# Three edits to a perceiver kernel: the first tile's border, the last self group, the first gate chunk

## The chip, the cores and the metric

The kernel runs on one core of a Trainium2 chip. The metric is the device time of one execution in microseconds (us); the time before the change is 1605.65 us, the median of 3 runs (1605.06 to 1606.41).

## The reference

One perceiver block in f32 over x of 64 batches x 32 queries x 512. Every part adds to x:

```python
x = x + xattn(layernorm(x), ctx_768)   # 16 heads of 64, 257 keys of 384 per batch, q @ k.T / 8, softmax, @ v, @ Wo + bo
x = x + attn(layernorm(x))             # 32 keys per batch, relative position bias, softmax, @ v, @ Wo
x = x + ffn(layernorm(x))              # gate, up: 512 -> 1408, silu(gate) * up, down: 1408 -> 512
```

In the ffn the input, the hidden and all three weights are rounded to 8 bits: the scale of an activation is its largest absolute value over the whole tensor, that of a weight row its own. So no gate product can start before the last token of the second residual is normed and its maximum taken.

## The kernel before

The 2048 tokens are 16 tiles of 128 (4 batches each) and 4 groups of 4 tiles. The stages follow each other: the query projections of all groups (the result, `qk_by_tile`, goes to DRAM and comes back a tile at a time as `raw`); cross attention tile by tile (tile 0 "first", tile 1 "second", tiles 2 to 14 a loop, tile 15 "last", then a tail); self attention group by group; the ffn. f32 products are done as three products of high and low parts, so each operand is split: ScalarE (ACT) copies the high part, VectorE (DVE) subtracts to get the low part. Each engine's instructions stand in a written order, and semaphores join the engines: `filled` and `drained` count the uses of each of the 8 PSUM banks (s0, s1, t0, t1, o0, o1, q0, q1).

A cross tile works on four batches b = 0 to 3. For each, TensorE (PE) does four score products (L651, one bank each), transposes the probabilities of the batch before (L662), multiplies them with that batch's context (L674, three pieces, called PV here), and transposes the context of the batch ahead (`ctxT`, L620, chunks 0, 1, 2 in banks t0, t1, t0). DVE takes row maxima (L1151), splits the transposed probabilities (L935, pT) and contexts (L935, cT), scales half of the probabilities (L1159, norm) and adds the last key's part to PV's result (L1136, attended). GpSimd (POOL) subtracts each batch's last key from its context (`pool_less_last`, L1258) and splits the context into high and low (`pool_split`, L1273 and L1276). SyncE (SP) issues every DMA, in order, from one queue.

At the border of two tiles (b = 3) the next tile's `raw` is split into `qk`: four pieces rg = 0 to 3, high by ACT (L797), low by DVE (L1070, `dve_qk_low`). The score products of the next tile wait for these pieces (`s_qlo`) and, for rg = 0, for the three cT chunks. In tile 0 the order at the border is its own, since no output projection (`pe_wo`, L702) of a tile before stands there: `qk_next and not begun` in `dve_cross_tile`.

In the self part a group's last step goes over its tiles i = 0 to 3: `pe_self_attended` (L1505, 64 small products into four banks), products for later v (`pe_self_v`, L1491), `pe_self_out` (L1520, 24 products of 512 columns). The result of attended must be split by ACT and DVE into `aT2` before the out product reads it; there is one `aT2`. DVE then adds the residual (`x_res2`, one tile, loaded by SP) in `dve_self_out` (L1725), and norms. In the last group the norms go straight to `xn3_all`, while the 12 tiles of the earlier groups come back from DRAM in one load (L1929).

In the ffn `pe_gate_up` does 11 chunks of gate and up products for 512 tokens (L1963), three rounds in a loop and a last one. The tokens come in two halves of 256, each transposed by PE (L1951) into q0 and q1; for the first round DVE copies half 0 to `xqT` (L2093) and ACT half 1 (L2029). Before its first product a round waits for both:

```python
            for b in ("q0", "q1"):
                pe.wait_ge(drained[b], U3.before(b, n, section, 1))
```

## Time and profile before

| | |
|---|---|
| median of 3 runs | 1605.65 us (1605.06 to 1606.41) |
| profiled execution, its own time | 1601.76 us |
| its span, first to last instruction | 1600.0 us |
| PE busy | 1548.1 us, 97% |
| DVE busy | 1072.9 us, 67% |
| ACT busy | 732.2 us, 46% |
| POOL busy | 372.2 us, 23% |
| mean granted TensorE clock | 0.988 |

PE is busy almost everywhere, so time is lost only where it stands still or runs at a lower granted clock. The page's row of 40 slices shows these places: the first slice, the slices from 160 to 240 us (end of the projections and tile 0 of cross attention), and 1440 to 1480 us (end of self attention and start of the ffn), where the granted clock is 0.79 of full speed in the mean.

### The profile page before, as it was taken

The page shows a single profiled execution, that of the slowest core. Times are in us where ns is not written, and L with a number is a line of the kernel's source. Part 1 is how long each engine was busy: PE and PEld are TensorE (multiplying, and loading weights), DVE is VectorE, ACT ScalarE, POOL GpSimd, SP SyncE. Part 2 cuts the span into 40 slices and gives each one's busy share as a digit, 9 for nine tenths or more (in the row PEclk, how much of TensorE's full clock was granted, in tenths as well). Part 3 has the DMA queues.
Part 4 walks back from the last instruction along what each step waited for, and adds up shares of the span by engine and source line. Part 5 has one row for each costly group of instructions (what it writes and reads, how often), then busy time and mean ns, then how long its engine had stood idle before and what let it go on. Part 6 is the DMA issues. An engine that isn't in the chain of part 4 may idle for free.

```text
span 1600.0 us, 36060 instructions
## 1 busy us (share of the span) xinstructions
PE 1548.1 (97%) x13778; PEld 1286.6 (80%) x13778; DVE 1072.9 (67%) x2314; ACT 732.2 (46%) x1589; POOL 372.2 (23%) x225
## 2 busy tenths in 40 slices
PE   7999879999999999999999999999999999996989
PEld 6888668888989899888989899878878788784444
DVE  7766677776667766776667766556565565555788
ACT  5544645555545554555545554433222222223755
POOL 1000343343444344343444344400000000000000
PEclk9999989999999999999999999999999999997999
DMA  6898862431333223331334223240311312242022
GB/s 245 319 366 327 330 243 109 137 135 59 138 132 140 74 106 136 136 134 59 138 134 138 76 104 122 97 181 22 120 54 40 114 41 66 100 157 97 1 105 106
DMA packets 80047, 213.63 MB, mean 134 GB/s; under 512 B 5776, under 2 KB 31824, under 8 KB 77136
## 3 DMA queue, kind: packets, MB, share of 16 engines
q1 hardware_dynamic: 79952, 212.27, 36.9%
q8 instruction: 71, 1.16, 0.3%
q14 instruction: 24, 0.20, 0.0%
HBM read 141.86 MB, written 70.39 MB: 133 GB/s over the span
## 4 chain that ended last, share of the span: by engine, by line
PE 74%; issue 11%; DVE 9%; ACT 4%; DMA 1%; POOL 0%; DVEq 0%; SPq 0%; ACTq 0%; POOLq 0%
PE psum_o L674 13%; PE psum_s L651 7%; PE psum_q L651 6%; PE psum_o L1451 6%; PE psum_q L1491 6%; PE psum_q L1451 6%; PE psum_t L1520 6%; PE psum_o L539 5%; PE psum_o L689 5%; DVE qk L1070 3%; PE psum_t L662 3%; PE psum_t L620 2%; PE psum_s L1478 1%; PE psum_t L571 1%; PE psum_q L571 1%
## 5 line engine op out<-in xcount | busy, mean ns | idle before, releaser
L674 PE MATMUL psum_o<-pT,c_nat 128*128 128x512 f32 x1152 | 307.3, 403 | 1.0 <-DVE pT L935 0.7
L674 PEld LDWEIGHTS psum_o<-pT,c_nat 128*128 128x128 f32 x1152 | 202.7, 188 | 36.1 <-DVE pT L935 1.0
L1273 POOL TENSOR_TENSOR c_nat<-c_raw,constants 128x768 fp32r<-128x768 f32 x64 | 94.9, 1483 | 574.4 <-PE psum_o L674 460.3
L1136 DVE TENSOR_SCALAR oT<-psum_o,c_last 128x512 f32<-128x512 f32 x192 | 143.9, 749 | 66.7 <-PE psum_o L674 66.6
L651 PE MATMUL psum_s<-cT,qk 128*128 128x256 f32 (+1 forms) x1152 | 168.8, 289 | 11.2 <-DVE cT L935 9.3
L651 PEld LDWEIGHTS psum_s<-cT,qk 128*128 128x128 f32 x1152 | 152.1, 191 | 20.3 <-DVE cT L935 14.1
L864 ACT ACTIVATE probs<-psum_s,nmax 128x257 f32<-128x257 f32 x128 | 61.1, 477 | 205.2 <-DVE nmax L1151 205.2
L651 PE MATMUL psum_q<-cT,qk 128*128 128x256 f32 (+1 forms) x1152 | 152.2, 283 | 0.7 <-DVE qk L1070 0.7
L651 PEld LDWEIGHTS psum_q<-cT,qk 128*128 128x128 f32 x1152 | 143.0, 190 | 3.5 <-issue 2.6
L935 DVE TENSOR_TENSOR pT<-psum_t,pT 128x512 fp32r<-128x512 f32 x128 | 87.8, 687 | 70.9 <-ACT pT L755 70.9
L1258 POOL TENSOR_TENSOR c_raw<-c_raw,last_row 128x768 f32<-128x768 f32 x64 | 120.2, 1879 | 22.2 <-DMA last_row<-in_ctx_dram 22.2
L755 ACT ACTIVATE cT<-psum_t 128x256 fp32r<-128x256 f32 x192 | 67.1, 387 | 115.3 <-PE psum_t L620 115.2
L1276 POOL TENSOR_TENSOR c_nat<-c_raw,c_nat 128x768 fp32r<-128x768 f32 x64 | 118.1, 1846 | 5.0
L1070 DVE TENSOR_TENSOR qk<-raw,qk 128x1536 fp32r<-128x1536 f32 x62 | 108.1, 1765 | 0.0
L2215 POOL PARTITION_ALL_REDUCE tiny<-tiny x1 | 0.4, 381 | 445.3 <-DVE tiny L2131 445.3
L797 ACT ACTIVATE qk<-raw 128x1536 fp32r<-128x1536 f32 x64 | 94.6, 1515 | 0.0
L689 PE MATMUL psum_o<-oT,wv 128*64 128x128 f32 x1536 | 87.4, 274 | 0.2 <-issue 0.2
L539 PE MATMUL psum_o<-xnT,wq 128*128 128x512 f32 x372 | 87.2, 393 | 0.0
L1520 PE MATMUL psum_t<-w2o_high,aT 128*128 128x512 f32 x256 | 83.0, 396 | 4.0 <-DVE aT L935 4.0
L689 PEld LDWEIGHTS psum_o<-oT,wv 128*64 128x64 f32 x1536 | 83.5, 137 | 2.4 <-issue 0.4
L1491 PE MATMUL psum_q<-w2v_high,xnT 128*128 128x512 f32 x256 | 84.6, 397 | 0.0
L539 PEld LDWEIGHTS psum_o<-xnT,wq 128*128 128x128 f32 x372 | 69.1, 188 | 17.1 <-issue 1.4
(273 smaller groups left out, 3120.3 us busy)
## 6 DMA issues: line engine op xcount, KB each, us to landing
qk_by_tile<-staged SPq DMA_DIRECT2D x32, 1536.0 KB, 10.2
raw<-qk_by_tile SPq DMA_DIRECT2D x16, 3072.0 KB, 12.3
c_raw<-in_ctx_dram SPq DMA_DIRECT2D x64, 384.0 KB, 3.2
last_row<-in_ctx_dram SPq DMA_DIRECT2D x64, 192.0 KB, 3.9
out_dram<-x_out SPq DMA_DIRECT2D x32, 256.0 KB, 2.0
x_res<-in_x_dram SPq DMA_DIRECT2D x16, 256.0 KB, 2.7
x_in<-out_dram SPq DMA_DIRECT2D x4, 1024.0 KB, 8.3
x_res<-out_dram SPq DMA_DIRECT2D x16, 256.0 KB, 2.9
```

The costliest lines, as they stand in the source:

```text
L539: m = pe.matmul(ps[:], wq[:, part, k, j * P:(j + 1) * P], xnT[:, moving, k, :, :], start=(k, part, moving) == (0, 0, 0), stop=(k, part) == ...
L651: m = pe.matmul(ps[:, 0:keys], qk[:, part, rg, c, b, :], cT[b % 2][:, moving, c, 0:keys], start=(c, part, moving) == (0, 0, 0), stop=(c, p ...
L674: i = pe.matmul(ps[:], c_nat[(b - 1) % 2][:, part, k, m * P:(m + 1) * P], pT[:, moving, k, :], start=(k, part, moving) == (0, 0, 0), stop= ...
L689: i = pe.matmul(ps[64 * par:64 * par + 64, h4 * P:(h4 + 1) * P], wv[:, c, head * DH:(head + 1) * DH], oT[:, c, slot, :, :], start=c == 0, ...
L1070: nc.vector.tensor_tensor(part[1], raw[:, :, rg, :].rearrange("p h (a q) -> p h a q", q=SQ), part[0].bitcast(F32), ALU.subtract).then_inc( ...
L1136: nc.vector.tensor_scalar(oT[:, m, :, (b - 1) % 4, :], ps[:].rearrange("p (s q) -> p s q", q=SQ), c_last[:, (b - 1) % 2, m:m + 1], None, A ...
L1258: nc.gpsimd.tensor_tensor(c_raw[i][:], c_raw[i][:], row_, ALU.subtract).then_inc(s_sub, 1)
L1273: G.tensor_tensor(flat(c_nat[i][:, 0, :, :]), flat(c_raw[i][:]), zero.to_broadcast([P, 2 * DC]), ALU.add).then_inc(s_chi, 1)
L1276: G.tensor_tensor(c_nat[i][:, 1, :, :], c_raw[i][:], c_nat[i][:, 0, :, :].bitcast(F32), ALU.subtract).then_inc(s_nat, 1)
L1451: m = pe.matmul(ps[:], (w2_high[w], w2_low[w])[part][:, k, j * P:(j + 1) * P], xnT2[:, moving, k, :, :], start=(k, part, moving) == (0, 0, ...
L1491: m = pe.matmul(ps[:], xnT2[:, part, k, i, :], w[moving][:, k, 512 * n:512 * (n + 1)], start=(k, part, moving) == (0, 0, 0), stop=(k, part ...
L1520: m = pe.matmul(ps[:], aT2[:, part, k, :], w[moving][:, k, :], start=(k, part, moving) == (0, 0, 0), stop=(k, part) == (KI - 1, 1))
```

## The change

Four things move; no product is added or taken away, except that some are cut in two.

1. Border of tile 0. DVE's order is new: piece 0 of `qk` first, then attended 0, chunks 0 and 1 of the context, piece 1, the norms, chunk 2, attended 1, pieces 2 and 3. ACT copies context chunk 2 ahead of pieces 2 and 3. In tile 1 POOL waits until all four `qk` pieces are split, and does `pool_less_last` of batch 1 ahead of `pool_split` of batch 0.
2. SP issues Wo, Wv, bo and x_res behind the context of batch 4 (tile 1's first).
3. Last self group. The last v product moves behind attended(2), out(2) is cut in two halves of 12 products, and attended(3) stands between them; tile 3 has a buffer of its own (`aT2_last`), and the residuals of tiles 2 and 3 come in one load (`x_res_last`). DVE does the probabilities of tile 3 earlier, and the norms of tiles 0 and 1 before the split of tile 3. Both buffers lie where `xn3_all` will be, so the load of the normed groups is cut: group 0 where all three stood, groups 1 and 2 behind the last tile's store, with a wait of its own on ACT before the gate loop.
4. Gate chunk 0 of each loop round is done in two passes of 256 tokens, and the first needs only half 0.

```diff
@@ act_cross_tile
+                if b == 3 and not begun:
+                    ctxT(b, 2)
...
-                if after:
+                if after and (b < 3 or begun):
                     ctxT(b, 2)
@@ dve_cross_tile
-                if qk_next and begun:
+                if qk_next:
                     dve_qk_low(dve, t + 1, 0, section)
                 dve_attended(dve, t, b, 0, section)
                 inverse(b, 3)
-                if qk_next and begun:
+                if qk_next and not begun:
+                    ctxT(b, 0)
+                    ctxT(b, 1)
+                    dve_qk_low(dve, t + 1, 1, section)
+                    norm(b, 2)
+                    norm(b, 3)
+                    ctxT(b, 2)
+                    dve_attended(dve, t, b, 1, section)
+                    dve_qk_low(dve, t + 1, 2, section)
+                    dve_qk_low(dve, t + 1, 3, section)
+                    dve_attended(dve, t, b, 2, section)
+                    continue
@@ pool_cross_tile
+                if section == "second" and b == 0:
+                    pool.wait_ge(s_qlo, 4 * t + 4)
+                    pool_less_last(pool, t, b + 1)
+                    pool_split(pool, t, b, section)
+                    continue
@@ sp_project_all
-            sp.dma_start(wo_raw[:], Wo.rearrange("(k p) n -> p k n", p=P)).then_inc(s_wo, 16)
             full(sp, U1(("CT", 0, 2), 0, "first"))
             sp.wait_ge(s_nat, 2)
             load_ctx(sp, 0, 3)
             load_qk(sp, 0, 1)
+            sp.wait_ge(s_nat, 3)
+            load_ctx(sp, 0, 4)
+            sp.dma_start(wo_raw[:], Wo.rearrange("(k p) n -> p k n", p=P)).then_inc(s_wo, 16)
             sp.dma_start(wv[:], Wv.rearrange("(k p) n -> p k n", p=P)).then_inc(s_wvo, 16)
@@ pe_self_all
+                if last:
+                    pe_self_attended(pe, s, 2)
+                    pe_self_v(pe, s, 3, 1)
+                    pe_self_out(pe, s, 2, range(KI // 2))
+                    pe_self_attended(pe, s, 3)
+                    pe_self_out(pe, s, 2, range(KI // 2, KI))
+                    pe_self_out(pe, s, 3)
@@ dve_self_all, last group
+                    dve_self_probs(dve, s, 3, ch)
+                    dve_self_out(dve, s, 1, ch2)
+                    dve_self_attended(dve, s, 2)
                     dve_out_rsqrt(dve, slice(0, 2), ch2)
                     dve_out_norm(dve, s, slice(0, 2), ch2)
+                    dve_self_attended(dve, s, 3)
+                    dve_self_out(dve, s, 2, ch2)
                     dve_short_rsqrt(dve, 2, ch2)
                     dve_out_norm(dve, s, slice(2, 3), ch2)
+                    dve_self_out(dve, s, 3, ch2)
@@ sp_self_all
                     if not more and i == 0:
+                        sp.dma_start(x_res_last[:], x1_dram[(TILES - 2) * P:, :].rearrange("(t p) d -> p t d", p=P)).then_inc(s_xres_last, 16)
...
+                        sp.dma_start(xn3_all[:, 0:GROUP, :].rearrange("p t d -> p (t d)"), xn3_dram[0]).then_inc(s_x3back, 16)
+                    if not more and i == GROUP - 1:
+                        sp.dma_start(xn3_all[:, GROUP:GROUP * (GROUPS - 1), :].rearrange("p (s t) d -> p s (t d)", t=GROUP),
+                                     xn3_dram[1:].rearrange("s p n -> p s n")).then_inc(s_x3later, 16)
@@ pe_gate_up
+            first = 1 if section == "loop" else 0
+            places = [empty(pe, U3(("GU"[w], i), n, section)) for i in range(first) for w in range(2)]
+            for half, b in enumerate(("q0", "q1")):
                 pe.wait_ge(drained[b], U3.before(b, n, section, 1))
+                for i in range(first):
+                    for w in range(2):
+                        ps, done = places[2 * i + w]
+                        m = products(i, w, ps, slice(256 * half, 256 * half + 256))
+                        if half:
+                            m.then_inc(done, 1)
@@ act_ffn
             act.wait_ge(s_out, 16 + 32 * TILES)
+            act.wait_ge(s_x3later, 16)
             with act.Fori(0, NCH - 1) as n:
```

How DVE's instructions stand at the border of tile 0, before (`qk` is a piece's low part, `cT_90` a context chunk, `probs_65` a norm, `oT` attended, `nmax` the next tile's first row maximum):

```order
269 L1155 RECIPROCAL rden<-den 128x1
270 L1136 TENSOR_SCALAR oT<-psum_o,c_last 128x16x32
271 L1155 RECIPROCAL rden<-den 128x1
272 L935 TENSOR_TENSOR cT_90<-psum_t,cT_90 128x256 x2
273 L1070 TENSOR_TENSOR qk<-raw,qk 128x4x12x32 x2
274 L1159 TENSOR_SCALAR probs_65<-probs_65,rden 128x256 x2
275 L1136 TENSOR_SCALAR oT<-psum_o,c_last 128x16x32
276 L1070 TENSOR_TENSOR qk<-raw,qk 128x4x12x32 x2
277 L935 TENSOR_TENSOR cT_90<-psum_t,cT_90 128x256
278 L1136 TENSOR_SCALAR oT<-psum_o,c_last 128x16x32
279 L1151 TENSOR_REDUCE nmax<-psum_s 128x1
```

And DVE at the same place after the change:

```order
269 L1163 RECIPROCAL rden<-den 128x1
270 L1078 TENSOR_TENSOR qk<-raw,qk 128x4x12x32
271 L1144 TENSOR_SCALAR oT<-psum_o,c_last 128x16x32
272 L1163 RECIPROCAL rden<-den 128x1
273 L943 TENSOR_TENSOR cT_90<-psum_t,cT_90 128x256 x2
274 L1078 TENSOR_TENSOR qk<-raw,qk 128x4x12x32
275 L1167 TENSOR_SCALAR probs_65<-probs_65,rden 128x256 x2
276 L943 TENSOR_TENSOR cT_90<-psum_t,cT_90 128x256
277 L1144 TENSOR_SCALAR oT<-psum_o,c_last 128x16x32
278 L1078 TENSOR_TENSOR qk<-raw,qk 128x4x12x32 x2
279 L1144 TENSOR_SCALAR oT<-psum_o,c_last 128x16x32
280 L1159 TENSOR_REDUCE nmax<-psum_s 128x1
```

The instructions are the same; one piece moved ahead of attended 0, and context chunk 2 from the end to a place before attended 1.

DVE in the last self group before, from the probabilities of tile 3 (`sum`, `pr`, `pT_1`) over out(2) (`x_out`) and the split of attended(3) (`aT_124`) to the norms of tiles 0 and 1 (`xn_all`):

```order
1024 L1701 TENSOR_REDUCE sum_129<-pr_114 128x16
1025 L1702 RECIPROCAL sum_129<-sum_129 128x16
1026 L1703 TENSOR_TENSOR pr_114<-pr_114,sum_129 128x512
1027 L1708 STREAM_TRANSPOSE pT_1_116<-pr_114 128x512
1028 L1725 TENSOR_TENSOR x_out_55<-psum_t,x_res_126 128x512
1029 L1727 BN_STATS out_stats<-x_out_55 128x6
1030 L935 TENSOR_TENSOR aT_124<-psum_s,aT_124 128x8x32 x2
1031 L935 TENSOR_TENSOR aT_124<-psum_o,aT_124 128x8x32 x2
1032 L1756 TENSOR_SCALAR xn_all<-x_out_55,out_ln 128x512 x2
1033 L1762 TENSOR_REDUCE xmax<-xn_all 128x1 x2
```

DVE there after the change; here `x_out` is that of out(1), and `aT_124` the split of attended(2):

```order
1003 L1739 TENSOR_REDUCE sum_129<-pr_114 128x16
1004 L1740 RECIPROCAL sum_129<-sum_129 128x16
1005 L1741 TENSOR_TENSOR pr_114<-pr_114,sum_129 128x512
1006 L1746 STREAM_TRANSPOSE pT_1_116<-pr_114 128x512
1007 L1769 TENSOR_TENSOR x_out_55<-psum_t,x_res_126 128x512
1008 L1771 BN_STATS out_stats<-x_out_55 128x6
1009 L943 TENSOR_TENSOR aT_124<-psum_s,aT_124 128x8x32 x2
1010 L943 TENSOR_TENSOR aT_124<-psum_o,aT_124 128x8x32 x2
1011 L1017 TENSOR_TENSOR out_ln<-out_stats 128x2
```

The probabilities of tile 3 moved ahead of out(1) and of the split of attended(2), which now stands before the reciprocal roots (`out_ln`) of tiles 0 and 1.

## Rows read from the trace of the kernel before

**Rows 1.** Waits of PE: waiting line, releaser, total us, times, longest.
```profile
PE psum_s L651 <- DVE cT L935: 9.3, 1, 9.3
...
PE psum_t L1520 <- DVE aT L935: 4.0, 2, 2.0
```

**Rows 2.** PE's timeline, tiles 0 and 1: start, us, line, idle before.
```profile
240.96 1.01 PE L651 MATMUL psum_s<-cT,qk 128*128 128x256 f32 x3 [9.29 <-DVE cT L935]
...
246.89 1.56 PE L674 MATMUL psum_o<-pT,c_nat 128*128 128x512 f32 x6
...
255.91 5.46 PE L689 MATMUL psum_o<-oT,wv 128*64 128x128 f32 x96
```

**Rows 3.** DVE's timeline at the border of tile 0.
```profile
225.13 0.16 DVE L1155 RECIPROCAL rden<-den 128x1 f32<-128x1 f32 x1 [0.18 <-ACT probs L864]
...
232.19 3.44 DVE L1159 TENSOR_SCALAR probs<-probs,rden 128x256 f32<-128x256 f32 x2
```

**Rows 4.** DVE's timeline at a border in the loop of tiles.
```profile
335.36 1.76 DVE L1070 TENSOR_TENSOR qk<-raw,qk 128x1536 fp32r<-128x1536 f32 x1
...
340.09 0.61 DVE L1159 TENSOR_SCALAR probs<-probs,rden 128x256 f32<-128x256 f32 x2
...
344.60 0.69 DVE L1144 TENSOR_TENSOR x_out<-psum_q,x_res 128x512 f32<-128x512 f32 x1
...
346.35 0.42 DVE L1151 TENSOR_REDUCE nmax<-psum_s 128x1 f32<-128x257 f32 x1
...
348.83 0.68 DVE L935 TENSOR_TENSOR pT<-psum_t,pT 128x512 fp32r<-128x512 f32 x1
```

**Rows 5.** The chain that ended last, in tile 0: start, us, what.
```profile
213.19 12.16 DMA last_row<-in_ctx_dram
```

**Rows 6.** POOL's timeline at the border of tile 0.
```profile
231.04 2.56 POOL L1273 TENSOR_TENSOR c_nat<-c_raw,constants 128x768 fp32r<-128x768 f32 x1 [3.79 <-PE psum_o L674]
...
235.44 1.85 POOL L1258 TENSOR_TENSOR c_raw<-c_raw,last_row 128x768 f32<-128x768 f32 x1
```

**Rows 7.** Windows of 2 us: busy per engine, then granted clock, DMA share, GB/s.
```profile
196.00:198.00 2.00, 0.14 (x2) 0.00 (x0) 1.33 (x4) 0.66 (x3) 2.00 (x2) 1.00 0.98 398
...
200.00:202.00 2.00, 2.00 (x11) 2.00 (x11) 0.95 (x2) 0.42 (x1) 0.00 (x0) 0.50 0.53 98
202.00:204.00 2.00, 2.00 (x15) 2.00 (x15) 1.29 (x5) 1.22 (x4) 0.00 (x0) 0.77 0.98 315
```

**Rows 8.** The chain that ended last, end of the last self group.
```profile
1430.89 5.44 PE psum_t L1520 x24
1436.33 2.72 PE psum_q L1491 x12
1442.50 7.07 PE psum_t L1520 x24
1452.96 5.72 PE psum_t L1520 x24
```

**Rows 9.** DVE's timeline in the last self group.
```profile
1437.82 0.16 DVE L1009 TENSOR_TENSOR out_ln<-out_stats 128x2 f32<-128x2 f32 x1
...
1441.61 0.75 DVE L935 TENSOR_TENSOR aT<-psum_o,aT 128x256 fp32r<-128x256 f32 x2
```

**Rows 10.** Timelines of DVE, ACT and PE where the gate products start.
```profile
1467.85 0.69 DVE L2093 COPY xqT<-psum_q 128x1024 bf16<-128x1024 bf16 x1 [0.34 <-PE psum_q L1951]
...
1468.80 1.02 ACT L2029 ACTIVATE xqT<-psum_q 128x1024 bf16<-128x1024 bf16 x1 [1.75 <-PE psum_q L1951]
...
1470.06 1.89 PE L1963 MATMUL psum_s<-xqT,wguT 128*128 x4 [1.39 <-ACT xqT L2029]
```

**Rows 11.** PE's timeline at the kernel's end, 512 and 256 columns.
```profile
1591.90 2.54 PE L1988 MATMUL psum_o<-wdT,hq 128*128 128x512 bf16 x11
1594.28 1.36 PE L2006 MATMUL psum_o<-wdT,hq 128*128 128x256 bf16 x11
```

**Rows 12.** The page's DMA issues: KB each, median us to landing.
```profile
x_in<-out_dram SPq DMA_DIRECT2D x4, 1024.0 KB, 8.3
```

More of the change, by code:

```diff
@@ L143, in self_units @@
                 u += [(("XT", s + 1, k), ("t1", "q0", "q1", "o0")[k]) for k in range(4)]
+            if i == 2 and s == 3:
+                u.append((("V2", s, 3, 1), "q1"))
             if i == 3 and s < 3:
                 u.append((("Q", s + 1, 0), "q0"))
[L146 removed]
+            u.append((("WO2", s, i), "t1" if (s, i) == (3, 3) else "t0"))
             if i == 0:
                 u.append((("V2", s, 2, 1), "q1"))
[L149 removed]
+            if i == 1 and s < 3:
                 u.append((("V2", s, 3, 1), "q1"))
@@ L1217, in dve_cross_tile @@
                     ctxT(b, 1)
-                if qk_next and not begun:
-                    dve_qk_low(dve, t + 1, 0, section)
-                    dve_qk_low(dve, t + 1, 1, section)
                 norm(b, 2)
@@ L1388, in sp_project_all @@
             sp.dma_start(x_res[:], rows(x_rows, 0)).then_inc(s_xres, 16)
-            for b in range(2, 4):
-                sp.wait_ge(s_nat, b + 1)
-                load_ctx(sp, 0, b + 2)
+            sp.wait_ge(s_nat, 4)
+            load_ctx(sp, 0, 5)
         def sp_cross_tile(sp, t, section):
@@ L1508, in pe_self_attended, with attended_of, pe_self_out @@
                         m.then_inc(places[b][1], 1)
-        def pe_self_out(pe, s, i):
+        def attended_of(s, i):
+            return aT2_last if (s, i) == (GROUPS - 1, GROUP - 1) else aT2
+        def pe_self_out(pe, s, i, ks=range(KI)):
             if (s, i) == (0, 0):
@@ L1514, in pe_self_out @@
             ps, done = empty(pe, own(("WO2", s, i)))
-            w = (w2_high["o"], w2_low["o"])
+            w, a = (w2_high["o"], w2_low["o"]), attended_of(s, i)
             for b in range(4):
                 taken(pe, own(("A2", s, i, b)))
-            for k in range(KI):
+            for k in ks:
                 for part, moving in PARTS:
-                    m = pe.matmul(ps[:], aT2[:, part, k, :], w[moving][:, k, :],
+                    m = pe.matmul(ps[:], a[:, part, k, :], w[moving][:, k, :],
                                   start=(k, part, moving) == (0, 0, 0), stop=(k, part) == (KI - 1, 1))
-            m.then_inc(done, 1)
+            if ks[-1] == KI - 1:
+                m.then_inc(done, 1)
         def pe_turn_weights(pe, c):
@@ L1566, in pe_self_all @@
                 pe_self_v(pe, s, 1, 1)
-                for i in range(GROUP):
+                last = s == GROUPS - 1
+                for i in range(2 if last else GROUP):
                     pe_self_attended(pe, s, i)
@@ L1663, in act_self_all @@
                     act_self_x(act, s + 1)
+                else:
+                    act_self_v(act, s, 3, 1)
                 act_self_attended(act, s, 3)
@@ L1719, in dve_self_out @@
             ps, free = full(dve, own(("WO2", s, i)))
-            dve.wait_ge(s_xres, 16 * t + 16 * (TILES + 1))
+            if t < TILES - 2:
+                dve.wait_ge(s_xres, 16 * t + 16 * (TILES + 1))
+                res = x_res2[:]
+            else:
+                dve.wait_ge(s_xres_last, 16)
+                res = x_res_last[:, t - (TILES - 2), :]
             if t == 0:
@@ L1955, in pe_gate_up, with products @@
         def pe_gate_up(pe, n, section):
-            for b in ("q0", "q1"):
-                pe.wait_ge(drained[b], U3.before(b, n, section, 1))
-            for i in range(FC):
+            def products(i, w, ps, part):
+                later = xqT[:, :, part.start:]
+                for k in range(KD):
+                    m = pe.matmul(ps[:, part], wguT[:, i, w, k, :], later[:, k, bass.ds(n * 512, part.stop - part.start)],
+                                  start=k == 0, stop=k == KD - 1)
+                return m
+            first = 1 if section == "loop" else 0
+            places = [empty(pe, U3(("GU"[w], i), n, section)) for i in range(first) for w in range(2)]
+            for half, b in enumerate(("q0", "q1")):
+                pe.wait_ge(drained[b], U3.before(b, n, section, 1))
+                for i in range(first):
[3 more added lines that the diff above has]
+                        if half:
+                            m.then_inc(done, 1)
+            for i in range(first, FC):
                 for w in range(2):
                     ps, done = empty(pe, U3(("GU"[w], i), n, section))
-                    for k in range(KD):
-                        m = pe.matmul(ps[:], wguT[:, i, w, k, :], xqT[:, k, bass.ds(n * 512, 512)],
-                                      start=k == 0, stop=k == KD - 1)
-                    m.then_inc(done, 1)
+                    products(i, w, ps, slice(0, 512)).then_inc(done, 1)
                 if i in (6, 8) and section == "loop":
```

47 lines of the change are left out of this document (24 added, 23 removed).

## The prediction, made before the changed kernel ran

> **What bounds the kernel now.** I read the page's 40 slices first: PE is busy 97% of the span, so only the few stretches where it stands still or runs at a lower clock can give time. The waits of PE name them: 9.3 us in one piece at L651 behind DVE's cT, and 4.0 us in two pieces at L1520 behind DVE's aT [rows 1]. Then the timelines around each wait say what ends last there.
>
> At the border of tile 0 PE stands 9.29 us and takes up the score products of tile 1 at 240.96; its first PV product of that tile comes at 246.89 [rows 2]. DVE is what ends last: from its reciprocal at 225.13 on it has four qk pieces, three contexts, two norms and three attended to do, and the context chunk that PE waits for stands near the end. One pair of norms took 3.44 us there [rows 3], against 0.61 us at a border in the loop [rows 4]; POOL was splitting and subtracting contexts from 231.04 to 237.29 [rows 6]. Ahead of that DVE waited for a context of which POOL's subtraction was late: its last-row transfer took 12.16 us [rows 5], issued behind Wo, raw, Wv, bo and x_res.
>
> At the end of the last self group two out products follow their attended directly, and each waits 2.0 us for the split. The first then runs 7.07 us, where the one before took 5.44: the clock had fallen. The last took 5.72 [rows 1, 8].
>
> At the start of the gate products PE waits 1.39 us for ACT's copy of half 1, though DVE's copy of half 0 had long ended [rows 10].
>
> **Part 1, the border of tile 0.** The new order is nearly that of the loop's border, so I take its length from there: from the first qk piece at 335.36 to the row maximum of the next tile at 346.35 are 10.99 us without a wait. This holds all that tile 0 must do and one step more, x_out (0.69): 10.3 us remain. From that row maximum to the end of the second pT (348.83 + 0.68) are 3.16 us [rows 4]. In tile 0 the first qk piece can start when the reciprocal ends, at 225.29 [rows 3]; its ACT half is done by then. So the row maximum comes at 235.6, pT ends at 238.75, and PV starts near 238.85 instead of 246.89 [rows 2]: 8.0 us less. PE's own work until there is shorter: it will stand in several short pieces, the longest between its fourth score product and PV, 2.5 to 3 us by DVE's time. What is late next is therefore DVE itself, not PE.
>
> POOL's three steps now wait for the fourth qk piece (about 235) and take at most what they took before, 6.25 us [rows 6]: until 241.3. PE's context transposes behind the first PV need only the first, the subtraction (1.85), by 237. The split is needed one batch later. Behind the waiting subtraction stands nothing but POOL's own splits; SP waits for the split before it loads the next context and the next raw, both needed a batch and a tile later.
>
> A clock term stands against this. [...] Of the two equal waits of 2.0 us for aT, one was followed by a slow product (7.07) and one was not (5.72) [rows 1, 8], so standing still for so long can go either way: the end without a fall is 0, the end with one 1.5, and I take the middle, 0.75. [...]
>
> Bounds of part 1: 8.0 + 0.5 above (the loop's steps are as short as they get); below, 3.7, the rival below.
>
> **Part 2, Wo and Wv later.** They go out near 213.6, behind the context that was late, so POOL's subtraction is ready when its turn comes and PE's transposes wait for nothing; this is in part 1's sum, as there DVE starts without a wait. Issued then, Wo and Wv are 3.5 MB, and the first product with Wv stood at 255.91 [rows 2], 248 now: 34 us away. The window at 196 moved 398 GB/s, that at 202 315 GB/s [rows 7], so they need 9 to 12 us. I cost this at nothing; the cover is those 34 us.
>
> **Part 3, the last self group.** The work is the same, 24 out products and the v product [rows 8]. What goes: two waits, 4.0 us [rows 1], the slow clock of the first out product, 7.07 − 5.44 = 1.63, and at most 0.28 of the second: 5.6 to 5.9. I take 5.6, as the two extra switches between kinds of product cost something. What must hold: attended takes 1.4 us (3.45 from 1439.05 to 1442.50, less a wait of 2.0). The split of attended(2) ended 3.31 us after attended started (1439.05 to 1442.36) [rows 8, 9]. Now attended(2) starts at 1436.33 and the split ends at 1439.65, as DVE is free from about 1437.8 (it started its roots then). The probabilities of tile 3, moved ahead of out(1), fall into the time in which DVE waits for out(1), which PE ends at 1436.33. The half product starts at 1436.33 + 1.4 + 2.8 = 1440.55: 0.9 us of slack. Behind it DVE has the roots, 1437.82 to 1440.9 [rows 9], 3.1 us, then two norms and maxima, some 2.3 us: until 1445.05. Attended(3) then starts at 1443.3, its split is due from 1444.8 and must end by 1447.5; it does by 1446.6, with 0.9 us to spare. If one slack fails, about 1 us is lost. If both fail and the clock falls again, 2.5 us: the lower end is 3.
>
> The load of the normed groups 1 and 2 (2 MB) now goes out behind the last tile's store: out ended at 1458.68 [rows 8], x_out takes 0.69 [rows 4], so less 5.6 it is 1453.8 on the old scale. ACT must have it before its first silu, which follows the first gate product, 1470.06 [rows 10] less 5.6, 1464.5. That leaves 10.7 us. Transfers moved 315 to 398 GB/s where they were alone [rows 7]: 5.3 to 6.7 us, plus some 2 us to start. I cost it at nothing.
>
> **Part 4, the first gate chunk.** DVE's copy of half 0 ends at 1468.54. PE started 0.24 us behind ACT's copy (1469.82 to 1470.06), so pass one can start at 1468.78 instead of 1470.06: 1.28 us less. It holds as many columns as four full products, 1.89 us at that clock [rows 10], so half 1 is there before it ends. Each loop round also does 16 products of 256 columns for 8 of 512: eleven of 512 take 2.38 from start to start, eleven of 256 at most 1.36 [rows 11]. A chunk costs at most 1.98 instead of 1.73, in two rounds 0.5 us. I take 1.2, with ends 0.5 and 1.9 (if the clock rises sooner because PE no longer stands for 1.39 us, up to half of that comes back).
>
> **The sum.** 8.0 − 0.75 + 0 + 5.6 + 1.2 = 14.05 us, say 14.1. Against the profiled execution's own 1601.76 (span 1600.0 and 1.76 around it) that is 1587.7. The median of the runs shown lies 3.89 above that execution; the same sum from 1605.65 gives 1591.55, and I predict 1591.5.
>
> **Rivals.** First, the border keeps part of its wait: POOL's work, now bunched behind the fourth qk piece, meets DVE's norms of tile 1's first batch. These come about 3 us behind PV, near 242, and POOL ends by 241.3, so 0.7 us parts them. If they meet, the pair takes 3.44 instead of 0.61 [rows 3, 4], 2.8 us, and the clock falls too, 0.75 more than the sum holds: 10.5 us remain, 1595.1. For it: exactly this pair was hit before. Against: before, POOL started 1.1 us ahead of it, now it is through. [...]
>
> Second, the normed load comes late. 1 MB of x_in took 8.3 us to land [rows 12], so 2 MB at that pace 16.6, 5.9 us later than ACT needs it. PE has three pairs of banks to run ahead, so at least part is hidden; I price it at 4: 1595.5. Against: x_in was loaded beside other transfers, and here only a store of 256 KB is ahead.
>
> Third, slower than before: the same load, but stuck like the last row (128 x 384 values of 4 bytes, 192 KB) that took 12.16 us [rows 5]. It decides from 25 us for the 2 MB on (10.7 plus the 14.1 of the sum), since behind ACT stands the whole gate stage. At the pace of that transfer with its context of twice the size, 576 KB in 12.16 us, 2 MB take 43 us: 1605.65 − 14.1 + 32.3 = 1623.9. For it: one queue issues everything, and the load moved behind a wait. Against: there is nothing else in the queue then; in the old place 4.2 MB were ahead of it.
>
> **How the numbers follow.** Forecast 0.70, first rival 0.16, second 0.11, third 0.03. The likeliest case has its own range, 1589 to 1594: no clock fall and a sooner gate clock at one end (15.5 to 16.5 us), one failed slack and a clock fall at the other. The range reaches 1597 for the two rivals that still gain, and 1587.5 below, for the upper ends of all three parts (8.5 + 5.9 + 1.9 = 16.3) and a spread between executions of some 1.4 us as in the three runs. About 0.2% (3.2 us) is what a measurement of this kernel can tell from no change: faster 0.95 (all cases but the third and the tails of the first two), within it 0.02, slower 0.03.
>
> **What would show it.** In the changed kernel's profile: the wait of 9.3 us at L651's successor is gone, PE's first PV of tile 1 comes near 239, DVE runs without a gap from 225.3 to the second pT, and the norms there take 0.3 us each. The two waits for aT are gone, the last out product ends some 5.6 us earlier relative to its group, at full clock. PE's first gate product starts about 0.2 us behind DVE's copy. ACT's first silu doesn't wait for a transfer. I am wrong if the norm pair shows 1.5 us or more apiece again, if PE waits for POOL's subtraction or split in tile 1, if a new wait for aT appears between the halves, or if ACT stands ahead of the gate loop for the normed load.

## The result, and the profile after

| | median | lowest to highest | executions |
|---|---|---|---|
| before | 1605.36 us | 1602.14 to 1606.41 | 4 |
| after | 1587.70 us | 1586.65 to 1589.14 | 4 |

The ratio is 0.9896 (95% interval 0.9882 to 0.9911), so 16.7 us less (14.3 to 18.9); the two medians alone lie 17.7 apart. The forecast of 1591.5 us (range 1587.5 to 1597.0) had the right sign and came 3.8 us too high: the median lies 0.2 inside the lower end of the range, and below the 1589 to 1594 that the prediction gave its likeliest case. The profiled execution of after took 1586.65 us, span 1584.9, mean granted clock 0.996; the sum had said 1587.7 for it. In the experiments below, one execution of the kernel with the gate passes alone took 8650.88 us, and the differences leave it out.

PE's waits after, the counterpart of [rows 1] (waiting line, releaser, total us, times, longest). Line numbers are 6 to 64 higher than before:

```profile
PE psum_s L532 <- DVE x_nrm L1040: 11.4, 1, 11.4
PE psum_q L2002 <- issue: 7.2, 1, 7.2
PE psum_q L2051 <- DVE hq L2146: 4.2, 1, 4.2
PE psum_t L668 <- issue: 2.5, 1, 2.5
PE psum_o L680 <- issue: 2.4, 1, 2.4
...
PE psum_t L1558 <- ACT wd_nat L1654: 1.4, 1, 1.4
```

The waits of 9.3 and 4.0 us are gone. New are 2.4 us at L680, the short stand ahead of PV in tile 1 that the prediction priced, and 1.4 us at L1558, where weights of the ffn are turned. The wait at L2002 is 7.2 where it was 6.1; from the last residual to the transposes are 8.10 us in both profiles, so PE only has less left to do in them.

**The border.** PE's timeline at the border of tile 0 (start, us, line, idle before), which answers to [rows 2]: the PV that opens the border, the first PV of tile 1, the first product with Wv.

```profile
225.08 1.53 PE L680 MATMUL psum_o<-pT,c_nat 128*128 128x512 f32 x6
...
239.51 1.64 PE L680 MATMUL psum_o<-pT,c_nat 128*128 128x512 f32 x6 [2.44 <-issue]
...
248.62 4.59 PE L695 MATMUL psum_o<-oT,wv 128*64 128x128 f32 x80
```

DVE's timeline there, which answers to [rows 3]:

```profile
225.97 1.76 DVE L1078 TENSOR_TENSOR qk<-raw,qk 128x1536 fp32r<-128x1536 f32 x1
...
230.74 0.61 DVE L1167 TENSOR_SCALAR probs<-probs,rden 128x256 f32<-128x256 f32 x2
...
232.26 3.42 DVE L1078 TENSOR_TENSOR qk<-raw,qk 128x1536 fp32r<-128x1536 f32 x2
...
236.25 0.41 DVE L1159 TENSOR_REDUCE nmax<-psum_s 128x1 f32<-128x257 f32 x1
...
238.73 0.68 DVE L943 TENSOR_TENSOR pT<-psum_t,pT 128x512 fp32r<-128x512 f32 x1
```

From the opening PV to tile 1's first PV are 14.43 us; before it was 22.57 (it stood at 224.32, its partner at 246.89 [rows 2]): 8.14 less. The norm pair takes 0.61 where it took 3.44 [rows 3]. From the first qk piece to the row maximum are 10.28 us (the prediction said 10.3), and to the end of the second pT 3.16 more, as it said. One of its signs did not come: DVE does not run without a gap, it stands 1.12 us for ACT's pT ahead of the first pT.

**The last self group.** The chain that ended last (start, us, what), which answers to [rows 8]: out(1), half of out(2), then the other half and out(3) in one piece of 36, and the residual that follows.

```profile
1425.11 5.44 PE psum_t L1546 x24
...
1434.92 2.72 PE psum_t L1546 x12
...
1439.06 8.47 PE psum_t L1546 x36
1447.55 0.70 DVE x_out L1769
```

From the start of out(1) to the last residual are 22.44 us. Before, out(1) started at 1430.89 and the last out product (1452.96, 5.72 long) ended at 1458.68 [rows 8], its residual at 1458.70: 27.81, so 5.37 less.

**The gate.** PE's timeline after: the transposes, the first product, and the seventh product of the chunk list (the first two stand in two passes each).

```profile
1455.65 1.86 PE L2002 MATMUL psum_q<-ident,xq_nat 128*128 128x128 bf16 x16 [7.25 <-issue]
1457.54 1.03 PE L2011 MATMUL psum_s<-xqT,wguT 128*128 x4
...
1464.04 1.03 PE L2011 MATMUL psum_s<-xqT,wguT 128*128 x4
```

The same two ends before:

```profile
1466.80 1.87 PE L1951 MATMUL psum_q<-ident,xq_nat 128*128 128x128 bf16 x16 [6.14 <-issue]
...
1478.21 1.03 PE L1963 MATMUL psum_s<-xqT,wguT 128*128 x4
```

Transposes to seventh product: 11.41 us before, 8.39 after, 3.02 less. The start of the first product gives 1.37 of it (3.26 behind the transposes before, 1.89 now). The rest of this pair, 1.65, is the clock. Windows of 2 us after (busy time per engine, then granted clock, DMA share, GB/s), and of before:

```profile
1458.00:1460.00 2.00, 2.00 (x11) 1.44 (x10) 0.00 (x0) 1.98 (x3) 0.00 (x0) 0.50 0.00 0
1460.00:1462.00 2.00, 2.00 (x13) 1.14 (x12) 0.59 (x1) 1.99 (x3) 0.00 (x0) 0.95 0.00 0
```

```profile
1474.00:1476.00 2.00, 2.00 (x6) 0.63 (x5) 0.56 (x1) 0.54 (x1) 0.00 (x0) 0.50 0.00 0
1476.00:1478.00 2.00, 2.00 (x11) 0.93 (x10) 0.75 (x1) 0.60 (x2) 0.00 (x0) 0.98 0.00 0
```

Before, the clock came back to full speed some 6 us behind the first product (1470.06 to 1476), after some 2.6 (1457.54 to 1460.1).

**Balance of the two profiles:** border −8.14, self group −5.37, gate −3.02; against it 0.76 more ahead of the border (PE's start-up wait, 10.8 before, 11.4 here, 10.8 to 11.9 in other profiles of this study, so scatter) and 1.5 more between the first product with Wv and out(1), most of it the 1.4 at L1558. That makes −14.3 of the −15.1 between the two spans. The rest, 0.8, lies at the first twelve down products, which no edit touches: from start to start they took 5.08 before and 4.27 after. The wait at L1558 has a partner in the profiles of two kernels with one part each (1.6 with the loads alone, 1.3 with part 3 alone) and none in that of border and loads together; what brings it stays open.

### The profile page after: what moved, and what is told of

Its sections match the earlier page's. It is cut to its first block, busy times and chain, and to the rows that moved or that the text cites. A ratio compares the mean times of both kernels' runs of the same rounds, so it can differ in the third digit from the quotient of the medians.

```text
span 1584.9 us, 36122 instructions
## 1 busy us (share of the span) xinstructions
PE 1543.2 (97%) x13802; PEld 1287.4 (81%) x13802; DVE 1069.9 (68%) x2314; ACT 732.4 (46%) x1589; POOL 369.0 (23%) x225
## 4 chain that ended last, share of the span: by engine, by line
PE 74%; issue 11%; DVE 9%; ACT 4%; DMA 1%; DVEq 0%; SPq 0%; ACTq 0%; POOLq 0%; POOL 0%
PE psum_o L680 13%; PE psum_s L657 7%; PE psum_q L657 7%; PE psum_q L1514 6%; PE psum_t L1546 6%; PE psum_o L1474 5%; PE psum_q L1474 5%; PE psum_o L545 5%; PE psum_o L695 5%; DVE qk L1078 3%; PE psum_t L668 3%; PE psum_t L626 2%; PE psum_t L577 1%; PE psum_s L1501 1%; PE psum_q L577 1%
## 5 line engine op out<-in xcount | busy, mean ns | idle before, releaser
L680 PE MATMUL psum_o<-pT,c_nat 128*128 128x512 f32 x1152 | 307.4, 403 | 3.4 <-issue 2.4
L680 PEld LDWEIGHTS psum_o<-pT,c_nat 128*128 128x128 f32 x1152 | 202.7, 188 | 38.7 <-DVE pT L943 3.6
L1275 POOL TENSOR_TENSOR c_raw<-c_raw,last_row 128x768 f32<-128x768 f32 x64 | 118.1, 1846 | 28.7 <-DMA last_row<-in_ctx_dram 18.3
L1474 PE MATMUL psum_o<-xnT,w2k_high 128*128 128x512 f32 x256 | 82.6, 403 | 0.0
```

Of the source, the lines that this page charges most:

```text
L680: i = pe.matmul(ps[:], c_nat[(b - 1) % 2][:, part, k, m * P:(m + 1) * P], pT[:, moving, k, :], start=(k, part, moving) == (0, 0, 0), stop= ...
L1275: nc.gpsimd.tensor_tensor(c_raw[i][:], c_raw[i][:], row_, ALU.subtract).then_inc(s_sub, 1)
L1474: m = pe.matmul(ps[:], (w2_high[w], w2_low[w])[part][:, k, j * P:(j + 1) * P], xnT2[:, moving, k, :, :], start=(k, part, moving) == (0, 0, ...
```

## The experiments

Differences are against the runs of the kernel before on the same chip, with 95% intervals; they are worked from the ratio over all executions, so they can differ by up to 1.3 us from the difference of the two medians. "PV to PV" is the distance from the PV that opens tile 0's border to tile 1's first PV: 22.57 before, 14.43 after.

### Each part alone

**Loads alone.** The kernel before with SP's edit as in the diff.

> The kernel before with part 2 alone: Wo, Wv, bo and x_res are issued behind the context that was late; the orders of DVE, ACT and POOL stay as they were. Theory A (the loads cost nothing, and the border's wait is set by DVE's order): the last-row transfer lands in 3 to 5 us instead of 12.16, PE no longer waits 1.45 for POOL's subtraction, and DVE takes up its qk pieces some 1.0 to 1.4 us earlier; the wait of 9.3 us shrinks by nothing or little and the run is 0.5 to 1.5 us faster. Rival B (the late context is what makes the border long): the wait of 9.3 falls below 6 and the run is 3 us or more faster. Rival C (Wo and Wv come late): slower by 1 us or more, with a wait ahead of the first product with Wv.

1603.14 against 1603.13 us: −0.2 (−1.6 to +1.3). Theory A's mechanism showed in part, with no time behind it: POOL's subtraction ended 2.0 us earlier (225.24 against 227.24 by its profile, whose opening PV is 0.65 later), PE's wait of 1.45 for it is gone, and DVE takes up its qk pieces 3.99 us behind the opening PV instead of 4.54, 0.55 sooner where 1.0 to 1.4 were expected. But PE still waits 9.3 for cT, and PV to PV is 22.43.

**Border order alone.** The kernel before with the edits of DVE, ACT and POOL.

> The kernel before with the new order on DVE, ACT and POOL at tile 0's border alone; SP's loads stay in the old order, so the last-row transfer is still late (12 us). Theory A: DVE begins with qk pieces, which don't need the context, and the late subtraction costs it only about 0.5 us where the contexts come: PE's first PV of tile 1 stands about 14.5 to 15.2 us behind the PV at the start of the border (22.57 before), the run is 6.8 to 8 us faster. Rival B (without the earlier context the new order keeps part of its wait): 4 us or less. Rival on the clock: if the new order lowers the granted clock, windows below 0.9 show between 228 and 245.

−3.8 us (−5.5 to −2.2): theory A is wrong, rival B right. The chain, then PE and DVE of this kernel, and DVE's wait for the same context before the change:

```profile
213.10 12.66 DMA last_row<-in_ctx_dram
```

```profile
228.59 0.81 PE L620 MATMUL psum_t<-ident,c_raw 128*128 128x128 f32 x4 [2.84 <-POOL c_raw L1269]
...
241.54 1.99 PE L674 MATMUL psum_o<-pT,c_nat 128*128 128x512 f32 x6 [2.44 <-issue]
```

```profile
229.49 0.79 DVE L937 TENSOR_TENSOR cT<-psum_t,cT 128x256 fp32r<-128x256 f32 x2 [1.88 <-ACT cT L755]
```

```profile
228.19 0.76 DVE L935 TENSOR_TENSOR cT<-psum_t,cT 128x256 fp32r<-128x256 f32 x2 [1.41 <-ACT cT L755]
```

The late last row holds POOL, POOL holds PE's context transposes, and DVE stands 1.88 us for the context that comes of them, where it stood 1.41 in the old order. PV to PV is 17.31 (224.23 to 241.54), not 14.5. The rival on the clock came true as well: from 230 to 232 and from 244 to 246 the granted clock is 0.50.

How much a late last row costs differs between executions. In the profile of the gate passes alone, whose border is the old one, it took 14.15 us; DVE stands 3.63 there for the context, and PV to PV is 26.30.

**Both together.**

> The kernel before with parts 1 and 2 together: the new order at tile 0's border and the later Wo and Wv. Apart they gave 3.2 us (order) and 0.0 (loads). Theory A (either alone leaves the other's wait in place: with the old loads DVE and PE wait for the late context, with the old order they wait for DVE's qk pieces; only together do both go): the PV of tile 1 comes 14.4 to 14.6 us behind the PV that opens the border, as in the changed kernel, and the run is 7 to 8.5 us faster than before. Rival (the parts add up, and the rest of the changed kernel's gain comes from parts 3 and 4): 3 to 4.5 us faster.

−7.4 us (−9.6 to −5.3); PV to PV is 14.43 in this profile too (223.51 to 237.94), 2.88 less than with the order alone. Alone the two give 0.2 and 3.8; each leaves the other's wait standing.

**Last self group alone.**

> The kernel before with part 3 alone: the last self group's half products, the x_res of the last two tiles in a place of their own, and the later load of the normed groups. Theory A: two waits of 2.0 and the slow product go: from the first out product of the group's tile 1 to the end of the last one 22.4 us instead of 27.8, the run 5.2 to 5.7 us faster; ACT waits for no transfer at the gate's start. Rival (the later load shows when nothing else moved): ACT's first silu waits, the gain is under 4.

−7.2 us (−9.5 to −5.0), in the median more than the 5.2 to 5.7 expected; the stretch itself is 22.8 us (1433.75 to 1456.52), and ACT waits for no transfer. What is removed differs between executions. Chains of the old order in two other kernels, the last two out products of 24 each, 5.44 at full clock:

```profile
1446.36 7.29 PE psum_t L1520 x24
...
1457.04 7.31 PE psum_t L1520 x24
```

```profile
1435.27 7.32 PE psum_t L1537 x24
...
1445.96 7.31 PE psum_t L1537 x24
```

Those are the gate passes alone, and border and loads: there the clock fell behind both waits, to 0.50 for some 3.5 us each time, which cost 3.7 us in all. In the profile that the prediction worked from it fell behind one (7.07 and 5.72 [rows 8], 1.9 in all), with the border order alone behind one (7.05), with the loads alone behind none. In these last two kernels the chain runs through another wait, the load of the residual, for which DVE stands ahead of the last split; here is that of the loads alone:

```profile
1440.12 11.41 DMA x_res<-out_dram
...
1454.50 5.72 PE psum_t L1521 x24
```

Part 3 takes this wait away too, as it loads the residuals of tiles 2 and 3 early and in one piece; the prediction did not name it. From the start of out(1) to the last residual the five profiles with the old order show 27.81, 27.03, 27.98, 29.62 and 29.65, 28.4 in the mean; the eight with the new one 22.36 to 22.79, 22.6 in the mean. So this stretch shows 5.8 us. The 1.4 between that and the 7.2 of the runs is not shown in it, and lies within the interval.

**Gate passes alone.**

> The kernel before with part 4 alone: the first gate product in passes of 256 columns. Theory A (work without a stand lifts the clock sooner): the first product starts 1.3 to 1.4 us earlier, and the granted clock is back at 1.00 some 3.5 us behind that start, not 6: the seventh gate product starts 3.0 us earlier than before, counted from the transposes' start (11.41 before); less up to 0.5 for the loop's extra products, the run is 2.4 to 3 us faster. Rival B (the sooner clock came from what lay ahead, the changed last self group): the clock comes back as long after the start as before, and the run is 0.8 to 1.3 us faster. Rival C (the passes cost more in the loop than they save): 0 to 0.8.

−2.2 us (−3.7 to −0.8). The seventh product comes 8.69 us behind the transposes (1472.48 to 1481.17; 11.41 before). The loop's passes cost nothing that shows: four half products of 256 columns start 0.44 apart, 1.75 for what took 1.73. So A, a little under its range in the median and inside it in the profile. The interval alone holds rival B's 0.8 to 1.3 too; the profile decides, as the granted clock is back some 3.3 us behind the first product, not 6.

The three pieces add up: 7.4 + 7.2 + 2.2 = 16.8 us, against 16.7 for the whole change, each piece known to some 1.5 to 2 us.

### POOL's old order in tile 1

```diff
-                if section == "second" and b == 0:
-                    pool.wait_ge(s_qlo, 4 * t + 4)
-                    pool_less_last(pool, t, b + 1)
-                    pool_split(pool, t, b, section)
-                    continue
                 pool_split(pool, t, b, section)
```

> The changed kernel with POOL's old order in tile 1: it splits the context as soon as the PV products free it (near 231) instead of waiting for the fourth qk piece. Theory A (POOL's steps meet DVE's norms and qk pieces, as in the kernel before): one or more of DVE's steps between 230 and 236 takes 1.6 us or more longer than in the changed kernel (norms 0.61 for two there), PV of tile 1 comes 1.5 to 3 us later, the run is 1.5 to 3 us slower than the changed kernel's 1587.7, so 13.5 to 15.5 us faster than before instead of 16.7. Rival (POOL's steps fall between those of DVE that they could delay): no DVE step longer by over 0.3 us, the time that of the changed kernel within 0.7.

1591.06 us, −13.2 (−15.4 to −11.1) against before, where the changed kernel has −16.7: 3.5 slower, past the 1.5 to 3 expected. DVE's norms and the last two qk pieces, then POOL, in this kernel:

```profile
230.31 1.82 DVE L1167 TENSOR_SCALAR probs<-probs,rden 128x256 f32<-128x256 f32 x2
...
233.04 5.76 DVE L1078 TENSOR_TENSOR qk<-raw,qk 128x1536 fp32r<-128x1536 f32 x2
```

```profile
232.06 1.83 POOL L1293 TENSOR_TENSOR c_nat<-c_raw,c_nat 128x768 fp32r<-128x768 f32 x1
233.84 3.34 POOL L1275 TENSOR_TENSOR c_raw<-c_raw,last_row 128x768 f32<-128x768 f32 x1
```

The norms take 1.82 for 0.61, the qk pair 5.76 for 3.42, and POOL's subtraction itself 3.34 for 1.83: norms and qk pieces ran beside steps of POOL, its subtraction beside the qk pieces. Attended, which DVE does between the two pairs at 232.39, beside POOL's split, took 0.73 (0.74 in after). PV to PV is 17.98 (224.66 to 242.64), 3.55 more than after, which is what norms (1.21) and qk pieces (2.34) lose. In this profile the clock fell behind the stand as well, to 0.50 from 242 to 248: from that PV to the first product with Wv are 11.61 us, against 9.11 in that of after.

### Why the gate's clock came back sooner

Two kernels from the changed one. First, both copies are waited for ahead of the passes:

```diff
-            for half, b in enumerate(("q0", "q1")):
+            for b in ("q0", "q1"):
                 pe.wait_ge(drained[b], U3.before(b, n, section, 1))
+            for half in range(2):
                 for i in range(first):
```

> The changed kernel with the first gate chunk still in passes, but each round waits for both copies before the first pass, as before the change. Theory A (the stand of 1.39 us itself delays the clock's return): the stand is back, the granted clock returns to 1.00 4 to 6 us behind the first gate product instead of 2.6, the seventh product starts 10 to 11.4 us behind the start of the transposes instead of 8.39, and the run is 1.8 to 3 us slower than the changed kernel. Rival B (the clock comes back a set time after the transposes, whatever stands between): the clock returns 4.5 to 5.5 us behind the transposes' start, as in the changed kernel, the seventh product comes 0.7 later at most, and the run is at most 0.8 us slower.

Second, the same, with the stand filled:

```diff
+            ps, _ = empty(pe, U3(("U", 2), 0, "loop"))
+            for k in range(3):
+                pe.matmul(ps[:], ident16[:], wguT[:, 0, 0, :, :], start=True, stop=True)
             with pe.Fori(0, NCH - 1) as n:
```

> As the run that waits for both copies, but PE fills the stand with three products whose result nobody reads (512 columns, into a bank that the third product overwrites). The real products start as late as there. Theory A (standing still delays the clock): the clock returns as soon behind the transposes as in the changed kernel, 4.5 to 5.5 us, the seventh product starts 8.8 to 9.4 us behind the transposes, and the run is 0.3 to 1 us slower than the changed kernel and 1 to 2 us faster than the run without the filler. Rival B (only when the real products start counts): as the run without the filler, within 0.4.

1590.55 us without the filler, 1587.64 with it. PE's transposes, first product and seventh product, of the one and of the other:

```profile
1457.54 1.86 PE L2002 MATMUL psum_q<-ident,xq_nat 128*128 128x128 bf16 x16 [7.25 <-issue]
1460.71 1.03 PE L2011 MATMUL psum_s<-xqT,wguT 128*128 x4 [1.30 <-ACT xqT L2093]
...
1468.22 1.03 PE L2011 MATMUL psum_s<-xqT,wguT 128*128 x4
```

```profile
1456.28 1.87 PE L2002 MATMUL psum_q<-ident,xq_nat 128*128 128x128 bf16 x16 [7.24 <-issue]
1458.37 1.06 PE L2044 MATMUL psum_t<-wguT,ident 128*128 128x512 bf16 x2 [0.22 <-issue]
1459.45 1.03 PE L2011 MATMUL psum_s<-xqT,wguT 128*128 x4
...
1465.47 1.03 PE L2011 MATMUL psum_s<-xqT,wguT 128*128 x4
```

The first real product comes 3.17 us behind the transposes in both. The seventh comes 10.68 behind them where PE stands 1.30, 9.19 where products that nobody reads fill that time. The granted clock is back at 1.00 some 7.9 us behind the transposes' start in the one, 4.9 in the other. Theory A holds: the stand itself put off the clock's return, and 1.5 us came back without any real work starting sooner.

One pair of profiles would be little, but the others agree. In six profiles PE stands ahead of the first gate product (before, loads alone, order alone, self group alone, border and loads, waits for both): the seventh product comes 9.80 to 11.41 us behind the transposes, the clock some 6 to 9.3. In four it does not (after, its repetition, gate passes alone, POOL's old order): 8.39 to 8.75, and 4.6 to 5.3. So what the stand costs differs from execution to execution, and the pair of the prediction's profile (11.41) and after (8.39) is the widest there is. The means of the kernels with the old gate (10.77, five profiles) and of those four (8.61) lie 2.16 apart, close to the 2.2 of the part alone.

The medians of the two kernels here lie 2.9 apart, more than expected, their profiled executions 3.6. Of these 1.49 is the gate, 0.89 lies ahead of the border, 0.85 behind the first down product and 0.36 between border and self group; at the last three places no edit parts the two.

### A faster version: no stand at four places

From the changed kernel, products whose result nobody reads at two places (ahead of the ffn's transposes, and between gate and down products):

```diff
+            pe.wait_ge(s_wguback, 32)
+            ps, _ = empty(pe, U3(("G", 0), 0, "loop"))
+            for k in range(28):
+                pe.matmul(ps[:], ident16[:], wguT[:, 0, 0, :, :], start=True, stop=True)
...
+            ps, _ = empty(pe, U3(("DN", 0, 0), 0, "down"))
+            for k in range(17):
+                pe.matmul(ps[:], ident16[:], wguT[:, 0, 0, :, :], start=True, stop=True)
```

> The changed kernel, and PE doesn't stand still in two places: 28 products of 512 columns whose result nobody reads run while the last reduction ahead of the gate stage is taken (PE stands 7.25 us there), and 17 such products in the 4.17 us between the gate and the down products. Theory A (PE's standing still is what lowers the clock there): the granted clock is 1.00 at the transposes, at the first gate products and at the first down products; the seventh gate product comes 6.3 to 7.0 us behind the transposes' start instead of 8.39, the first 12 down products take 2.7 to 3.2 us instead of 4.3, and the run is 2.5 to 4 us faster than the changed kernel. Rival B (the clock falls there whatever PE does, or DVE's and ACT's work ends last): within 0.7 of the changed kernel. Rival C (the filler stands in the way of the real work): slower by 0.5 to 2.

and at two more (tile 0's second batch ahead of its transposes, tile 1's first PV):

```diff
+        def keep_clock(pe, place):
+            ps, _ = empty(pe, place)
+            for k in range(40):
+                pe.matmul(ps[:, 0:P], ident16[:], ident16[:], start=True, stop=True)
...
+                    if (section, b) == ("second", 0):
+                        keep_clock(pe, U1(("PV", b, 0), t, section))
                     pe_pv(pe, t, b, 0, section)
```

> As the run that fills two places, and 40 products of 128 columns in each of two more: ahead of the transposes of tile 0's second batch (a stand of 2.5 us, after which the clock was 0.67 and 0.50 in the changed kernel), and ahead of tile 1's first PV product (a stand of 2.44; the changed kernel's profile shows no fall behind it, three later runs with the same border fell to 0.5 for some 3 us and lost 1.56). Theory A: the granted clock is 1.00 in all windows from 196 to 250, the second place gives 1.2 to 1.6 us, the third 0 to 1.6 by what would have happened without it; the run is 1.5 to 3 us faster than the one that fills two places. Rival B (DVE ends last at both places, so a faster PE gives nothing): within 0.7 of it.

> The changed kernel again, beside the two runs with fillers. Theory A: 16 to 18 us faster than before as in its first runs. On the border's clock: the theory that a stand of 2.44 us lowers the clock in some executions and not in others has the first product with Wv at either 23.5 (no fall) or 25.1 us (fall) behind the PV that opens the border, nothing between 24 and 24.7.

| beside each other on one chip | median | lowest to highest | against before |
|---|---|---|---|
| changed, again | 1587.99 us | 1584.73 to 1589.44 | −16.7 (−19.4 to −14.1) |
| two places filled | 1584.93 us | 1584.09 to 1586.36 | −18.6 (−21.3 to −16.0) |
| four places filled | 1582.73 us | 1582.38 to 1583.27 | −21.0 (−23.6 to −18.3) |

Two places were expected to give 2.5 to 4; it is 3.1 by the medians, 1.9 by the differences against before, and the executions overlap. With them the seventh gate product comes 7.07 us behind the transposes (expected 6.3 to 7.0; 8.39 and 8.60 in the two profiles of the changed kernel), and the first 12 down products take 2.71 from start to start (1540.53 to 1543.24) instead of 4.27 (1541.88 to 1546.15). Four places give 2.2 more by the medians, as expected (1.5 to 3). With them the mean granted clock of the execution is 1.000, and its slowest run is faster than the fastest of the changed kernel. PE at the border, of the kernel with four places and of the changed kernel again:

```profile
223.51 1.53 PE L680 MATMUL psum_o<-pT,c_nat 128*128 128x512 f32 x6
...
235.34 2.41 PE L715 MATMUL psum_o<-ident 128*128 128x128 bf16 x40
237.94 1.64 PE L680 MATMUL psum_o<-pT,c_nat 128*128 128x512 f32 x6 [0.19 <-issue]
...
247.04 5.46 PE L695 MATMUL psum_o<-oT,wv 128*64 128x128 f32 x96
```

```profile
225.35 1.53 PE L680 MATMUL psum_o<-pT,c_nat 128*128 128x512 f32 x6
...
239.78 2.02 PE L680 MATMUL psum_o<-pT,c_nat 128*128 128x512 f32 x6 [2.43 <-issue]
...
250.45 5.46 PE L695 MATMUL psum_o<-oT,wv 128*64 128x128 f32 x96
```

Both have 14.43 from PV to PV; to the first product with Wv it is 23.53 with the filler and 25.10 without. So the second expectation on the border's clock held: 23.5 or 25.1, nothing between.

## Why the prediction was right or wrong, point by point

- **Part 1, the length of the border: right.** 8.0 forecast, 8.14 measured, by the steps as priced. The saving depends on the execution that it is taken from: PV to PV of the old border was 23.05 and 26.30 in two further profiles.
- **Part 1, the clock term: its ends were right, the middle never occurs.** It is 0 or 1.56 us; no run shows the 0.75. The 1.5 of the upper end is what the two windows of rows 7 at 0.50 and 0.77 lack to full clock, 1.0 and 0.46 us. Other profiles agree for that place: from the transposes of tile 0's second batch, ahead of which PE stands 2.5 us, to the first PV behind them are 5.65 us before, where the clock fell to 0.50, and 4.13 with the gate passes alone, where it stayed at 1.00. At the border, of six profiles with the new order and no filler there (after and its repetition, border and loads, the two kernels on the gate's stand, the one with two places filled) one shows 0 and five show 25.10 or 25.11 us to Wv, a fall to 0.50 for some 3 us. So 1.56 is the likelier value, and the profile of after was the exception; that it lay close to the sum is in part luck. What decides a single execution stays open.
- **Part 2 at nothing: right as a sum, and incomplete as a reason.** The loads alone are worth 0.2, but 3.6 of the border's 7.4 hang on them (7.4 less the order's 3.8; PV to PV gives 2.88). The prediction had that inside part 1, where nobody could see that the order alone is worth half.
- **Part 3: right.** 5.6 forecast, 5.37 in the profiled pair, 5.8 between the means of all profiles. The switch between kinds of product, which the forecast counted at no set sum, shows as 0.23 us: twelve v products took 2.95 behind attended and 2.72 behind an out product before, and 2.95 behind attended after. The 7.2 (5.0 to 9.5) of its own runs is higher. That the old order's clock fell twice explains the surplus only in part: it did so in two of five profiles, and behind one wait or none in the other three.
- **Part 4: the term that was mis-sized.** 1.2 was forecast; its own runs gave 2.2, the means of the profiles 2.16, the profiled pair 3.02. The start gave 1.37, as priced, and the loop's cost, priced up to 0.5, is 0.02 a round. The clock gave the rest, 0.8 in the mean and 1.65 in the pair, where the prediction had put it only into its upper end ("up to half of that comes back", 0.7).
- **First rival (POOL meets the norms): did not occur.** POOL's first step there came at 235.75 and the last ended at 240.91; the norms of tile 1 at 242.65 took 0.61. With POOL's old order a meeting returned, and it cost 3.55 us. That this is the price given (2.8 + 0.75) is luck: it was paid by the norms and qk pieces of the border itself, not by the norms of tile 1 and the clock.
- **Second and third rival (normed load late): did not occur.** ACT's first silu (1460.47) followed its table load of 1.28 us without a wait for a transfer; the 2 MB had landed near 1456, 7.6 us behind their issue, where the prediction's 5.3 to 6.7 and 2 to start make 7.3 to 8.7. For that start the page of before shows 1.5 us for a transfer of 2 KB.

The gain of 16.7 is 2.7 over the sum of 14.05. The parts' own runs (7.4, 7.2, 2.2) put 0.15 of that at the border (7.25 forecast), 1.6 in the self group and 1.0 in the gate. The means of the profiles give 8.1 for the border up to the first product with Wv (33.0 in the three with the old order and the old loads, 24.8 in the six above), 5.8 and 2.2, so 0.9, 0.2 and 1.0. Both put the gate 1.0 above its term; on the other two they differ, by no more than the intervals of the runs allow, and that division stays open.

## What to carry to other kernels

Price a stand of PE twice: by its length and by the slow products behind it, and look at several profiles, since the second price is paid in some executions and not in others (here 0 or 1.56 us behind a stand of 2.4). Where PE must stand, as during a reduction, a few products that nobody reads can save the slow products behind the stand: at four places they gave some 4 to 5 us beyond the 16.7. Where two edits touch one wait, try each alone and both together: here 0.2 and 3.8 made 7.4.

## What the runs showed of the hardware

- A stand of 1.3 to 1.8 us ahead of the first gate product, while the granted clock was at 0.50, put off its return to 1.00: some 6 to 9.3 us behind the transposes in six profiles with the stand, 4.6 to 5.3 in four without. Three filler products in it brought 1.5 us back.
- Stands of 2.0 to 2.5 us from full clock were followed by 0.50 in some executions and not in others, at the same place of the same program; the loss was then 1.4 to 2.5 us. With fillers at four places the granted clock was 1.00 at each of them.
- A last-row transfer of 192 KB took 12.2, 12.7 and 14.2 us behind Wo, raw and Wv (median of all 64: 3.9); DVE then stood 1.41, 1.88 and 3.63 us for the context that hangs on it.
